# Graph attention with eight heads: Prelu for the logits, division by row sums on GpSimd, head outputs summed in PSUM

## The reference

```python
q = feat_proj @ q_w + q_b                      # a number per node
k = feat_proj @ k_w + k_b
logits = q + jnp.swapaxes(k, -1, -2)           # 512 x 512
masked = logits + (1.0 - adj_mat[:, None]) * NEG
masked = jax.nn.leaky_relu(masked, negative_slope=0.01)
attn = jax.nn.softmax(masked, axis=-1)
out = attn @ feat_proj
# heads side by side, then
out = out @ fp_w + fp_b + feats
return jax.nn.sigmoid(out)
```

## Time and profile before

| | us |
|---|---|
| median of 3 runs | 2728.84 (2728.32 to 2730.79) |
| span of the profiled execution | 2729.4 |
| PE busy | 2342.8 |
| DVE busy | 1942.6 |
| ACT busy | 1489.7 |
| POOL busy | 1056.6 |

### The profile page before, as it was taken

The page is one execution under the profiler, slowest core; times in us unless marked ns, Lnnn a source line. Parts: engine busy times, 40 slices in busy tenths (PEclk is TensorE's granted clock), DMA queues, the critical chain, the costliest instruction groups (busy, mean ns, idle before and its releaser), DMA issues.

```text
span 2729.4 us, 39618 instructions
## 1 busy us (share of the span) xinstructions
PE 2342.8 (86%) x12504; PEld 1816.8 (67%) x12504; DVE 1942.6 (71%) x5118; ACT 1489.7 (55%) x2854; POOL 1056.6 (39%) x861
## 2 busy tenths in 40 slices
PE   4888988799888998889988799887998879978899
PEld 3776667665686656867568575685756857668565
DVE  4987549875598745977469773697737977389773
ACT  2855438554485534846358463583636836367352
POOL 1751227512374124731247313472135721256211
PEclk7998899988898988989889898898998989989899
DMA  3010000100001000010000100001000010101000
GB/s 126 2 40 31 16 25 1 40 31 16 25 1 40 32 16 25 1 39 32 16 25 2 39 32 31 9 11 45 16 32 9 32 38 2 35 6 40 1 1 8
DMA packets 46845, 66.02 MB, mean 24 GB/s; under 512 B 3856, under 2 KB 21392, under 8 KB 46352
## 3 DMA queue, kind: packets, MB, share of 16 engines
q1 hardware_dynamic: 46608, 63.11, 6.9%
HBM read 58.91 MB, written 4.19 MB: 23 GB/s over the span
## 4 chain that ended last, share of the span: by engine, by line
PE 34%; issue 29%; POOL 28%; DVE 7%; ACT 2%; POOLq 1%; DMA 0%; SPq 0%; DVEq 0%; ACTq 0%
POOL U L301 16%; POOL tiles L301 7%; PE banks L351 7%; PE banks L353 6%; PE banks L352 6%; PE banks L579 6%; PE banks L635 2%; POOL rstd L281 2%; DVE hN L1023 1%; POOL adjN L289 1%; PE banks L655 1%; PE banks L556 1%; PE banks L608 1%; POOL PT L325 1%; POOL PT L340 1%
## 5 line engine op out<-in xcount | busy, mean ns | idle before, releaser
L301 POOL TENSOR_TENSOR U<-U,tiles 128x512 f32<-128x512 f32 x352 | 449.2, 1277 | 382.9 <-ACT tiles L755 377.0
L476 PE MATMUL banks<-F,PT 128*128 128x128 f32 x4096 | 546.4, 278 | 0.0
L476 PEld LDWEIGHTS banks<-F,PT 128*128 128x128 f32 x4096 | 503.5, 194 | 0.3
L755 ACT ACTIVATE tiles<-U,Q 128x512 f32<-128x512 f32 x352 | 251.2, 714 | 169.7 <-DVE kmax L1083 169.5
L460 PE MATMUL banks<-ident,U 128*128 128x128 f32 x1408 | 221.3, 282 | 105.9 <-ACT U L765 101.8
L823 ACT ACTIVATE F<-banks,dcols 128x512 f32<-128x512 f32 x288 | 198.2, 688 | 152.6 <-PE banks L353 137.4
L1122 DVE COPY PT<-banks 128x512 f32<-128x512 f32 x384 | 261.1, 682 | 23.7 <-PE banks L460 23.5
L765 ACT ACTIVATE U<-U,nmx 128x512 f32<-128x512 f32 x352 | 250.2, 711 | 18.3 <-DVE nmx L1108 18.3
L460 PEld LDWEIGHTS banks<-ident,U 128*128 128x128 f32 x1408 | 165.6, 145 | 125.4 <-issue 107.4
L1083 DVE CUSTOM_DVE_ANT_0 U<-adjN,banks 128x512 f32<-128x512 f32 x352 | 237.7, 675 | 10.1 <-issue 10.1
L281 POOL TENSOR_TENSOR rstd<-var,mhalf 128x4 f32<-128x4 f32 x66 | 74.2, 1128 | 416.4 <-DVE var L1018 416.4
(11 more groups left out here) (205 smaller groups left out, 5257.2 us busy)
## 6 DMA issues: line engine op xcount, KB each, us to landing
adjN<-in_adj_dram SPq DMA_DIRECT2D x32, 1024.0 KB, 5.4
adjT<-in_adjt_dram SPq DMA_DIRECT2D x16, 1024.0 KB, 5.3
xin<-in_x_dram SPq DMA_DIRECT2D x18, 256.0 KB, 6.0
out_dram<-X SPq DMA_DIRECT2D x16, 256.0 KB, 2.3
F<-in_c2w_dram SPq DMA_DIRECT2D x1, 1088.0 KB, 7.5
F<-in_wraw_dram SPq DMA_DIRECT2D x1, 1024.0 KB, 9.5
U<-in_fcw_dram SPq DMA_DIRECT2D x1, 512.0 KB, 3.7
U<-in_fpw_dram SPq DMA_DIRECT2D x1, 512.0 KB, 4.5
```

Source lines behind the costliest of these rows:

```text
L301: pool.tensor_tensor(SC[u % 3][:, t, :], SC[u % 3][:, t, :], RELU[:, t, :], ALU.add)\
L476: last = pe.matmul(B[s][:, 2 + h % 2, part(j)], PT[s][:, k, part(j)], G[s][:, k, h * DIM:(h + 1) * DIM], start=(k == 0), stop=(k == TILES ...
L755: act.activation(RELU[:, t, :], SC[u % 3][:, t, :], ACT.Relu, bias=Q99[s][:, t, h:h + 1], scale=99.0)\
```

## The change

It does five things:

- **Signs and Prelu.** Keys and mask are negated, so DVE forms the row minimum of the negated scores and writes it as a 513th column beside the scores (SC buffers grow to 513 columns). ACT `negated_logits(u, t)` applies Prelu (scale 0.01, alpha 100) in place to all 513 columns, which gives the negated logits and their row minimum together. The exponential takes its bias from column 513. RELU, `lift`, `kmax_q`, `neg_max` and `exp_bias` go, and SC has four buffers.
- **Division ahead of the transposes.** DVE's reciprocals of unit v are formed in DVE turn v+1 behind the mask of tile 1, and POOL `normalized(u)` multiplies the four tiles by rden (attn). The first transposes of unit u wait for attn in place of exped.
- **One bank for all heads.** The 8 heads of a slot accumulate in bank 2; one `output_sum(s)` adds it to acc at the end in place of 16 `add_head`. Bank 3 of each slot is free and serves two of the four stripes (`pt_bank`), so each stripe has its own bank.
- **Copies one turn later.** DVE and ACT copy the stripes of unit u-2 in turn u, where it was unit u-1. `key_rows(u + 3)` stays where it was in PE phase u. The turns of DVE and ACT run to UNITS + 1.
- **Loops written out.** The 8 rounds stand in the program one after the other on every engine. POOL's x + 0.5 (`x_half`) stands ahead of the first unit instead of behind the fifth and sixth. Setup weights are loaded to PT in place of U.

```diff
+        SC = [UX[0], UX[1], tiles[0], tiles[1]]
+        NSC = len(SC)
...
-            with pool.Fori(0, ROUNDS) as it:
+            for it in range(ROUNDS):
...
+                def normalized(u):
+                    s, turn = u % SLOTS, it * HEADS + u // SLOTS
+                    pool.wait_ge(*after("rden", turn, s))
                     for t in range(TILES):
-                        lift(u, t)
+                        pool.tensor_scalar(SC[u % NSC][:, t, 0:NODES], SC[u % NSC][:, t, 0:NODES], rden[s][:, t:t + 1], 1.0,
+                                           ALU.mult, ALU.mult).then_inc(S["attn"], 1)
...
                             if j == 0:
-                                pe.wait_ge(*after("exped", turn, s))
-                            if j >= 2:
-                                pe.wait_ge(*tile_out(turn, s, j - 2))
-                            elif u >= 1:
-                                pe.wait_ge(*tile_out(it * HEADS + (u - 1) // SLOTS, (u - 1) % SLOTS, j + 2))
+                                pe.wait_ge(*after("attn", turn, s))
+                            if u >= 1:
+                                pe.wait_ge(*tile_out(it * HEADS + (u - 1) // SLOTS, (u - 1) % SLOTS, j))
...
                             for k in range(TILES):
-                                last = pe.matmul(B[s][:, 2 + h % 2, part(j)], PT[s][:, k, part(j)],
-                                                 G[s][:, k, h * DIM:(h + 1) * DIM], start=(k == 0), stop=(k == TILES - 1))
+                                last = pe.matmul(B[s][:, 2, part(j)], PT[s][:, k, part(j)], G[s][:, k, h * DIM:(h + 1) * DIM],
+                                                 start=(h == 0 and j == 0 and k == 0),
+                                                 stop=(h == HEADS - 1 and k == TILES - 1), skip_group_check=True)
...
-                    act.activation(RELU[:, t, :], SC[u % 3][:, t, :], ACT.Relu, bias=Q99[s][:, t, h:h + 1], scale=99.0)\
-                        .then_inc(S["relu"], 1)
+                    act.activation(SC[u % NSC][:, t, :], SC[u % NSC][:, t, :], ACT.Prelu, bias=QN[s][:, t, h:h + 1],
+                                   scale=0.01, alpha=100.0).then_inc(S["logits"], 1)
...
-                for u in range(-1, UNITS + 1):
+                for u in range(-1, UNITS + 2):
                     for t in range(TILES):
                         if u + 1 < UNITS:
-                            relu(u + 1, t)
+                            negated_logits(u + 1, t)
                         if 0 <= u < UNITS:
                             softmax_exp(u, t)
-                        if t == TILES - 1 and 0 <= u - 1 < UNITS:
-                            tile_copy(u - 1, t)
+                        if t == TILES - 1 and 0 <= u - 2 < UNITS:
+                            tile_copy(u - 2, t)
...
-                        if t < TILES - 1 and 0 <= u - 1 < UNITS:
-                            tile_copy(u - 1, t)
-                    if 0 <= u - 1 < UNITS:
-                        denominators(u - 1)
-                    if u + 1 < UNITS:
-                        kmax_q(u + 1)
+                        if t < TILES - 1 and 0 <= u - 2 < UNITS:
+                            tile_copy(u - 2, t)
                     if u + 2 < UNITS:
                         masked_keys(u + 2, 0)
-                    if u + 1 < UNITS:
-                        neg_max(u + 1)
-                    if 0 <= u - 2 < UNITS:
-                        add_head(u - 2, 0)
-                    if u + 1 < UNITS:
-                        exp_bias(u + 1)
-                    if 0 <= u - 2 < UNITS:
-                        add_head(u - 2, 2)
```

More of the change, by code:

```diff
@@ L68 @@
     "mask0": 1, "qk_banked": 1, "qk": 1, "g_banked": 8, "g_act": 4, "g_dve": 4,
-    "kb_banked": 1, "masked": 4, "relu": 4, "lifted": 4, "kmax_q": 1, "neg_max": 1, "exp_bias": 1, "exped": 4,
+    "kb_banked": 1, "masked": 4, "logits": 4, "exped": 4, "attn": 4,
     "pt_banked": 4, "pt_dve": 3, "pt_act": 1,
-    "rden": 1, "o_banked": 1, "o_added": 1,
-    "acc_start": 1, "x_half": 1, "tanh0": 1,
+    "rden": 1, "o_banked": 1,
+    "acc_start": 1, "o_added": 1, "x_half": 1, "tanh0": 1,
     "mask1": 1, "h1_banked": 1, "h1_high": 1, "h1": 1, "h1_low": 1, "t1_banked": 1, "t1_high": 1, "t1_low": 1, "h1n_banked": 1,
@@ L154, in build @@
         kmax = [sb(f"kmax{s}", [P, TILES]) for s in SL]
-        kq = [sb(f"kq{s}", [P, TILES]) for s in SL]
         nmx = [sb(f"nmx{s}", [P, TILES]) for s in SL]
@@ L410, in _ @@
             values(0, 0, 0)
-            with pe.Fori(0, ROUNDS) as it:
+            for it in range(ROUNDS):
                 def transpose_out(s, layer, y):
@@ L743, in _ @@
                 h_high(s, 0)
-            with act.Fori(0, ROUNDS) as it:
+            for it in range(ROUNDS):
                 def g_copy(s, t):
@@ L761, in softmax_exp @@
                     turn = it * HEADS + h
-                    if t == 0:
-                        act.wait_ge(*after("exp_bias", turn, s))
-                    act.wait_ge(*after("lifted", turn, s, t + 1))
-                    act.activation(SC[u % 3][:, t, :], SC[u % 3][:, t, :], ACT.Exp, bias=nmx[s][:, t:t + 1], scale=0.01,
+                    if t == 0 and h >= 1:
+                        act.wait_ge(*after("rden", turn - 1, s))
+                    act.wait_ge(*after("logits", turn, s, t + 1))
+                    act.activation(SC[u % NSC][:, t, 0:NODES], SC[u % NSC][:, t, 0:NODES], ACT.Exp,
+                                   bias=SC[u % NSC][:, t, NODES:NODES + 1], scale=-1.0,
                                    accum_out=den[s][:, t:t + 1]).then_inc(S["exped"], 1)
@@ L1039, in _ @@
                 h_low(s, 0)
-            with dve.Fori(0, ROUNDS) as it:
+            for it in range(ROUNDS):
                 def add_residual(s, layer):
```

134 lines of the change are left out of this document (49 added, 85 removed).

## The result

| | before | after |
|---|---|---|
| median of 4 runs each, us | 2729.8 (2728.3 to 2733.7) | 3296.8 (3285.4 to 3302.9) |
| span of the profiled execution | 2729.4 | 3283.6 |
| DVE busy | 1942.6 | 1618.6 |
| POOL busy | 1056.6 | 736.2 |
| PE busy | 2342.8 | 2547.8 |

The change costs 567 us: 1.2066 times the time of before (95% interval 1.2041 to 1.2092). The forecast was 3403, the range 3083 to 3562. The kernel became slower, by the mechanism forecast, and the forecast was 106 us too high.

The account below looks back on a forecast made before the run. DVE was taken to bound layer 0 at 7.07 us per unit; the change would make a 13.6 us waiting cycle through PE and ACT. 2729.4 + 688 - 14 for loops = 3403 us, range 3083 to 3562.

Parts of the forecast that it names:

- to the first copy of stripe 3: Layer 0, from ACT's start on unit 2 at 409.0 to its first stripe 3 copy, forecast at about 421.5.
- twelve rings: Layer 0, key rows 4 to 15: the waiting cycle closes 12 times a round at 13.6 us, 163.2 us.
- The ring: Layer 0: ACT's copy, PE's products and key rows, DVE's mask, ACT's four pairs in series; 10.9 us per unit at full clock.
- The clock's share: Layer 0: PE's clock falls after its idle gap, once per unit, adding 2.7 us to 10.9.
- clock stays up: Rival for layer 0: PE keeps full clock, 10.9 us per unit, 3111 us in all; chance 0.15.
- Prelu: ACT in layer 0: Prelu over 513 columns priced as Relu over 512; four pairs take 5.30 us.
- the rival of 4640 us: ACT in layer 0: Prelu and exponential need different function tables, two loads of 1.28 us per pair; chance 0.01.
- POOL's multiplication: POOL in layer 0: each one-input multiplication with a per-partition factor takes 0.62 us, 2.5 us per unit.
- The rival's price: POOL in layer 0: multiplications at 1.28 us each add 0.9 us per unit, 3497 us in all; chance 0.10.
- The loops: Round starts: writing the loops out removes DVE's jump-back idle time, 2.0 us in 7 of 8 rounds, -14 us.
- at most some 4 us a round: Round starts: a shorter gap may keep PE's clock up in the value products; counted only in the range.
- Layers 1 to 3 keep their instructions and times: Layers 1 to 3: claimed no change in instructions or time, 171.4 us per round as before.

Follow-up runs that it names:

- experiment 1: Changed kernel with PE's key rows made one unit earlier, nothing else different: 2607.8 us, 0.956 times before.
- experiment 4: Kernel before with loops written out and PE's key rows one phase later, none of the change's arithmetic: 3135.3 us.
- experiment 6: Changed kernel with ACT's copy of stripe 3 back in its old turn and the reciprocals at the start of DVE's turn: 2957.2 us, 1.083 times before.
- experiment 3: Changed kernel with stripe 3 transposed four extra times on PE in phases 1 to 14, filling its pause with useless work: 3169.6 us.
- experiment 5: Changed kernel with POOL's four multiplications per unit written as two-input operations with a broadcast factor: 3357.5 us in one run.
- experiment 2: Kernel before with its five loops over the rounds written out and nothing else: 2683.1 us, 0.983 times before.

## Why the prediction was right in kind and 106 us high

The second round, term by term, each time from the end of the one ahead:

| term, us | before | predicted | measured |
|---|---|---|---|
| from POOL's adjN to ACT's unit 2 | 47.0 | 45.0 | 39.5 |
| to the first copy of stripe 3 | 5.7 | 12.5 | 12.6 |
| twelve rings | 107.6 with the next | 12 x 13.6 = 163.2 | 161.7 (13.48 each) |
| from the last ring's copy to the end of the products | (above) | 23.2 | 22.7 |
| to the next transposes | 2.8 | 3.3 | 2.3 |
| layers 1 to 3 | 171.4 | 171.4 | 164.0 |
| round | 334.5 | 418.6 | 402.8 |

**The ring** stood as predicted, link by link: ACT idle 7.25 us ahead of the Prelu (8 predicted), released by the mask, that one by PE's key rows, PE's first product by ACT's copy. Experiment 1 opens it and experiment 4 builds one by the place of the key rows alone; experiment 6 opens it by the copy's turn, with the reciprocals moved along. Four pairs took 5.29 us (507.61 to 512.90; 5.30 predicted).

**The clock's share** was 2.7 by two gaps of the kernel before; 13.48 - 11.15 = 2.3 by experiment 3, in which the ring without the fall was 0.25 longer than the sum had it. The two misses go opposite ways, so that 13.6 came within 0.1 of 13.48 is in part luck. The rival "clock stays up" (3111 us) is refuted by the changed kernel's clock of 0.75 over the stretch.

**Prelu** was priced as Relu, 0.71 us: it took 0.71. The list of ACT's instructions has one table load of 1.28 us in the whole execution, as before, so the rival of 4640 us is out. The Trainium skill (ScalarE: Activation LUTs, Table sets: the hidden batching unit) does not name Prelu among the functions that it lists for the exponential's set. The trace decides: 512 Prelus, 480 of them directly ahead of an exponential, and no load between them.

**POOL's multiplication** was taken as 0.62 between 0.62 and 1.28: it is 0.692 as one operation and 2.69 us for four. It is off the path, as predicted. The rival's price was wrong too: experiment 5 shows 1.04 for the two-input form and 0.18 us per unit, against 0.9.

**The loops** are the term that was mis-sized: -14 us, with up to 28 more left for the range. Experiment 2 measured -47 on the kernel before. The step multiplied one gap of 2.0 by 7 rounds. Measured were 3.7 us in the second round, and from the third on 6.7, since the clock then stays up behind QK: 3.0 more, which is the "at most some 4 us a round" that the prediction kept for the range.

**"Layers 1 to 3 keep their instructions and times"** is the step that failed. They kept their instructions, and lost 7.4 us in the second round, 5.4 to 7.4 in each of the first seven and 52 in all. From the first transposes behind layer 0 to POOL's adjN, PE alone (us, busy, clock), of the kernel before, of experiment 2, of experiment 1 and of the changed kernel:

```profile
525.20:696.50 171.30, 155.73 (x571) 0.89 0.06 19
```
```profile
517.80:688.80 171.00, 154.73 (x571) 0.90 0.06 19
```
```profile
508.80:675.90 167.10, 151.12 (x570) 0.92 0.06 19
```
```profile
673.90:837.90 164.00, 148.23 (x570) 0.94 0.06 20
```

The length follows the clock: 0.89, 0.90, 0.92, 0.94 for 171.3, 171.0, 167.1, 164.0 us. The loops have no part in it: in experiment 2 the stretch stays at 171.0 to 171.2 us in rounds two to seven. The head of the round is another matter. Of the 7.5 us that it lost, experiment 2 gives back 6.7 from its third round on by the loops alone, with the clock in the value products at 1.00, where it was 0.65 before. The prediction saw this possibility for the head and not for the layers. By its own terms: 5.5 us at the head, 1.9 in the ring and tail, 1.0 at the end and 7.4 in the layers are 15.8 us per round, seven of them 111 of the 119 us by which the forecast lies above the span of the profiled execution.

What stays open is why the clock falls in one place and not in another where PE's instructions and pauses are alike (experiment 5 against the changed kernel at the head of the round, the equal rings of experiment 4). No run here tells it.

## What to carry to other kernels

When a step moves to a later turn, follow who waits for it through every in-order queue until the path comes back to the step: where that ring is longer than any engine's own work, its length is the new period, and one entry on a third engine's list, moved by a turn, can open it (here 689 us). A queue order tuned for one chain of work is not tuned for a shorter one; after taking work off an engine, look at each wait that the old bound had hidden, then at the next engine's waits in the same way (2608 to 2555 us). And time off an unchanged stage is not safe: sum the changed stages, but leave a range for the clock in the others.

## What the runs showed of the hardware

PE's granted clock depends on more than a stretch's own work. In layer 3 of the second round, PE without any pause fell to half clock in the kernel before and not in the changed one, where the same instructions run 144.7 us later (us, busy, clock, share and GB/s of the transfers):

```profile
660.00:667.00 7.00, 7.00 (x22) 1.00 0.00 0
667.00:674.00 7.00, 7.00 (x15) 0.52 0.27 89
```
```profile
804.70:811.70 7.00, 7.00 (x22) 1.00 0.00 0
811.70:818.70 7.00, 7.00 (x28) 1.00 0.42 138
```

The fall came in the kernel before while PE had been busy for all of the last 7 us. Transfers ran beside it at 89 GB/s, but they are neither enough for the fall nor needed for it: the changed kernel had 138 GB/s at that place and kept the clock, and in the last round of the kernel before, which has no transfers there, the clock fell at the same place all the same:

```profile
2674.30:2681.30 7.00, 7.00 (x16) 0.51 0.00 0
```

On GpSimd one input of 128x512 with a factor per partition costs 0.69 us, with constants 0.62, a second input that is one broadcast column 1.04, and a full second input 1.28. The Trainium skill (GPSIMD Engine Reference, 4.1 Engine selection) has two classes only: one input roughly at line rate, two inputs about twice as slow as on VectorE. The trace agrees with it at both ends (0.62, and 1.28 beside the 0.68 of DVE's mask, which also has two inputs) and puts the two forms with a factor between them.
